# A graph kernel's attention layers: target scores spread behind the group's last sums

## The chip, the cores and the metric

The program runs on one core of a Trainium2 chip. The metric is device time in microseconds (us) of one execution; lower is better. A core has TensorE (PE: matmuls, PEld: its weight loads), VectorE (DVE), ScalarE (ACT), GpSimd (POOL, which here issues the gathers), SyncE (SP, which issues the other DMAs) and 16 DMA engines that all queues share.

## What is computed

Seven message-passing layers over a graph of 3125 nodes and 53125 edges, sorted by target node, with 256 features and layer norms between: one 8-head attention layer with edge features, four layers that sum or average, and two 4-head attention layers. The change touches only these last two:

```python
z = (x @ W).reshape(n, HEADS, ODIM)                  # HEADS = 4
el = jnp.sum(z * al, axis=-1)
er = jnp.sum(z * ar, axis=-1)
e = leaky_relu(el[src] + er[dst], negative_slope=0.2)
e_max = segment_max(e, dst, num_segments=n)
ex = exp(e - e_max[dst])
denom = segment_sum(ex, dst, num_segments=n)
msg = z[src] * (ex / denom[dst])[:, :, None]
out = segment_sum(msg, dst, num_segments=n) + x + b
```

## The kernel before

The edges are cut into 416 tiles of 128, and these into 52 groups of 8 tiles. A 4-head layer goes through its 52 groups in a software pipeline; each engine has its own program, in an order written out by hand, and the engines meet at semaphores.

**Gathers.** GpSimd issues eight indirect DMAs a group (L1819), one a tile. Each fetches 128 rows of 264 numbers (z and the source scores) from the layer's table into one of four row buffers. It waits for `rows_free`, which VectorE raises when a group has been added up (L1469). So, in step g, the buffer of group g-1 comes free, and the gathers of group g+3 start.

**Step g**, in which group g is summed and group g+1 is prepared:

- VectorE (`step` in `gat_dve`, L1471): `edge_scores(g+1)` adds the target scores, which lie in PSUM (`er_ps`), to the source scores in the gathered rows (L1387) and takes the leaky relu (L1388). It waits for the rows of group g+1 and for `er_ready`. Then the first half of `messages(g)` (L1425) multiplies z by the weights, once ScalarE has made them (`ex_ready`). `add_group(g-1)` adds the window of the group before (L1440, L1442), once TensorE has turned its sums (`sum_ready`), and raises `rows_free`. Then `scans(g+1)` (L1393, L1394: running maxima), the second half of `messages(g)`, `carry(g+1)` (L1400 to L1406: maxima that reach over tiles; waits for TensorE's L686), `rescale_node(g)` (L1434, L1436), `maxima(g+1)` (L1411 to L1417; the last one raises `shift_ready`) and `turned_hots(g+2)` (L1380).
- `turned_hots` compares the broadcast target numbers of a group's edges (`high_rows`, loaded by SP at L1740 with the tables of the group) with the partition number, and so makes the group's turned one-hots in bf16 (`turned_hot`, a part of the tile `attr`).
- TensorE (`step` in `gat_pe`, L741): `turn_scores(g+1)` (L681), the sums of group g over its eight tiles in three pieces (L711), between them `edges` (L686) and `carries` (L693) of group g+1, then `turn_back(g+1)` (L698), which turns the shifted scores for ScalarE and raises `back_ready`, then `spread_scores(g+2)` (L675): 24 matmuls of bf16, 8 tiles by 3 parts, with the turned one-hots as weights, which bring each edge's target scores into `er_ps`; the last raises `er_ready`. Then `rescales(g+1)` (L705), which waits for `ex_ready`, and `turn_sums(g)` (L724, L725), which raises `sum_ready`.
- ScalarE (`step` in `gat_act`, L1008): a copy for `near`, the one-hots of the sums, the copy of the group's sums (L1014, waits for the last L711), and `weights(g+1)`: L996, then the two exponentials L999 and L1000, which wait for `back_ready` and raise `ex_ready`.
- SP loads the tables of group g+3 once `maxima(g+1)` is done: penalties (L1733, L1737), then `high_rows` (L1740).

Of the kernel before, what the change touches and what calls it, by code (L numbers as in the profile page):

```python
# [82 lines left out]
def is_last(g):  # L83
    return isinstance(g, int) and g == NG - 1


def gnn_program(nc, a, out, stop):
    last_stage = NL - 1 if stop is None else stop
    ctx = ExitStack()
    with ctx:  # L90
# [252 lines left out]
        def wait_alone(eng, s, value):  # L343

            eng.wait_ge(s, value)
            eng.sem_inc(passed, 1)
# [110 lines left out]
        def tables_landed(eng, l, par, h):  # L457

            eng.wait_ge(seg_landed[par], SEG_BEFORE[l] + SEG_LOADS[l] * (h + 1))

        def next_group(j, h, ahead):

            return (j + ahead) % SUM_BUFS, h + (j + ahead) // SUM_BUFS

        def pair_of(j, h):

            return j % 2, 2 * h + j // 2
# [193 lines left out]
        def gat_pe(pe, l, turns, sum_turns):  # L661
# [6 lines left out]
            def spread_scores(n, j, h):  # L668

                par = j % 2  # L670
                pe.wait_ge(turned_hot_ready, gl + n + 1)
                pe.wait_ge(near_copied, gl + n + 1)
                for k in range(T):
                    for part in range(PARTS):
                        ins = mm(er_ps[:, k * H:(k + 1) * H], turned_hot[:, par, k, :],  # L675
                                 near[:, par, k, part * H:(part + 1) * H], start=part == 0, stop=part == PARTS - 1)
                ins.then_inc(er_ready, 1)

            def turn_scores(n):
                wait_alone(pe, al_ready, ag + n + 1)  # L680
                nc.tensor.transpose(alT_ps[0:TH, :], al3[:, 0:TH], ident[:, :]).then_inc(alT_ready, 1)  # L681

            def edges(n):
                wait_alone(pe, scans_ready, ag + n + 1)
                for j, ends in ((0, fwd[0:TH + 1, P - 1:P]), (1, bwd[0:TH + 1, 0:1])):
                    ins = mm(edge_ps[:, j * H * SLOTS:(j + 1) * H * SLOTS], ends,  # L686
                             perm[:, j, :, :].rearrange("p h s -> p (h s)"), start=True, stop=True)
                ins.then_inc(last_ready, 1)

            def carries(n):  # L690
                wait_alone(pe, carry_ready, ag + n + 1)
                for j in range(2):
                    ins = mm(carry_ps[0:TH, j:j + 1], carry_th[:, j, 0:TH], one[:, :], start=True, stop=True)  # L693
                ins.then_inc(carryT_ready, 1)

            def turn_back(n):
                wait_alone(pe, shift_ready, ag + n + 1)
                nc.tensor.transpose(back_ps[:, 0:TH], shifted[0:TH, :], ident[0:TH, 0:TH]).then_inc(back_ready, 1)  # L698

            def rescales(n, par):  # L700
                if not (isinstance(n, int) and n == 0):
                    pe.wait_ge(rescaled, ag + n)
                wait_alone(pe, ex_ready, ag + n + 1)
                for f in range(FC):
                    ins = mm(gat_resc_ps[:, f:f + 1], head_of[H][:, f, :], resc_h[par][0:H, :], start=True, stop=True)  # L705
                ins.then_inc(resc_ready, 1)

            def sum_tiles(par, b, ks):

                for k in ks:  # L710
                    ins = mm(gat_node_ps[par], gat_hot[par][:, k, :], src_rows(l, b)[:, k, 0:D + H],  # L711
                             start=k == 0, stop=k == T - 1)
                return ins

            def sums(g, b, half, ks):
                if ks[0] == 0:
                    pe.wait_ge(onehot_ready, ag + g + 1)
                pe.wait_ge(msg_ready, 2 * (ag + g) + half + 1)
                return sum_tiles(b % 2, b, ks)
# [7 lines left out]
            def turn_sums(g, b):  # L727
                par = b % 2
                pe.wait_ge(node_copied, NG * l + g + 1)
                pe.wait_ge(windows_done, NG * l + g - 1)  # L730
                turned(par).then_inc(sum_ready, 1)

                def window(w):
                    pe.wait_ge(more_ready, turns.now() + 1)
                    sum_tiles(par, b, range(T)).then_inc(more_nodes, 1)
                    pe.wait_ge(more_copied, sum_turns.now() + 1)
                    turned(par).then_inc(more_summed, 1)
                    turns.next()
                    sum_turns.next()
                further_windows(pe, g, window)  # L740

            def step(g, h, j):
                n = None if is_last(g) else g + 1
                if n is not None:
                    turn_scores(n)
                sums(g, j, 0, range(0, 4))
                if n is not None:
                    edges(n)
                sums(g, j, 1, range(4, 6))
                if n is not None:  # L750
                    carries(n)
                sum_tiles(j % 2, j, range(6, 8)).then_inc(node_ready, 1)
                if n is not None:
                    turn_back(n)
                    if not is_last(n):
                        spread_scores(n + 1, *next_group(j, h, 2))
                    rescales(n, (j + 1) % 2)
                turn_sums(g, j)

# [14 lines left out]
            spread_scores(1, 1, 0)  # L774
            rescales(0, 0)
            gat_loop(pe, step)

        def node_pe(pe, s):
# [588 lines left out]
        def gat_dve(dve, l, ch, turns, sum_turns):  # L1367
# [8 lines left out]
            def turned_hots(n, j, h):  # L1376

                par, turn = pair_of(j, h)
                tables_landed(dve, l, par, turn)
                V.tensor_scalar(turned_hot[:, par, :, :].rearrange("p t e -> p (t e)"), high_row[:, par, :], rank[:, 0:1],  # L1380
                                None, ALU.is_equal).then_inc(turned_hot_ready, 1)

            def edge_scores(n, b, h):

                rows_landed(dve, l, b, h)
                dve.wait_ge(er_ready, gl + n + 1)
                ch.then(V.tensor_tensor(grid(al), er_ps.rearrange("p (t h) -> p t h", h=H), src_rows(l, b)[:, :, D:D + H], ALU.add))  # L1387
                V.scalar_tensor_tensor(al3[:, 0:TH], al[:, 0:TH], 0.2, al[:, 0:TH], ALU.mult, ALU.max).then_inc(al_ready, 1)  # L1388
# [8 lines left out]
            def carry(n, par):  # L1397
                dve.wait_ge(last_ready, ag + n + 1)
                pr = gat_pen_row[0:1, par * 2 * HS:(par + 1) * 2 * HS]
                V.tensor_tensor_scan(carry_row[0:1, 0:HS], pr[:, 0:HS], edge_ps[:, 0:HS], -BIG, ALU.add, ALU.max)  # L1400
                ch.then(V.tensor_tensor_scan(carry_row[0:1, HS:2 * HS][:, ::-1], pr[:, HS:2 * HS][:, ::-1],
                                             edge_ps[:, HS:2 * HS][:, ::-1], -BIG, ALU.add, ALU.max))
                V.tensor_copy(perm[TH:TH + 1, 0, :, 0:1],
                              carry_row[0:1, 0:HS].rearrange("o (h s) -> o h s", h=H)[:, :, T:SLOTS])
                into = carry_row[0:1, 0:2 * (HS + 1)].rearrange("o (j x) -> o j x", j=2)[:, :, 0:HS]
                V.tensor_copy(carry_th[:, :, 0:TH].rearrange("o j (t h) -> o j h t", h=H),  # L1406
                              into.rearrange("o j (h s) -> o j h s", h=H)[:, :, :, 0:T]).then_inc(carry_ready, 1)
# [63 lines left out]
            def step(g, h, j):  # L1471
                n = None if is_last(g) else g + 1
                b, hn = next_group(j, h, 1)
                if n is not None:
                    edge_scores(n, b, hn)
                messages(g, j, 0)
                if not (isinstance(g, int) and g == 0):
                    add_group(g - 1, (j - 1) % 2)
                if n is not None:
                    scans(n, b % 2)  # L1480
                messages(g, j, 1)
                if n is not None:
                    carry(n, b % 2)
                rescale_node(g, j % 2)
                if n is not None:
                    maxima(n, b % 2)
                    if not is_last(n):
                        turned_hots(n + 1, *next_group(j, h, 2))

            edge_row = perm[TH:TH + 1, :, :, :]  # L1490
            V.memset(fwd[TH:TH + 1, :], 1.0)
# [10 lines left out]
            ch.flat()  # L1502

            gat_loop(dve, step, ch, GAT_STEPS)
            add_group(NG - 1, 1)

# [514 lines left out]
```

## Time and profile before

| | |
|---|---|
| median of 3 runs | 5965.95 us (5960.23 to 5992.97) |
| the profiled execution | 5953.5 us |
| its span | 5951.7 us |
| mean granted TensorE clock | 0.726 of full speed |
| busy: PE, PEld, DVE, ACT, POOL | 58%, 40%, 34%, 19%, 49% of the span |

Times in the rows are us from the span's start. The two 4-head layers run from about 4100 on: group after group, the first from 4144, the second from about 5045. An engine's name with a q behind it is its queue: DVEq L1469 is the semaphore increment of that line. Where a release is "remote", the profile found no instruction or DMA that gave it; "issue" means that the engine waited for nothing that the profile shows.

### The profile page before, as it was taken

To read this page: it belongs to the slowest core of one execution; us is meant where nothing else is said; L and a number is where in the kernel's file an instruction comes from. 1 tells how busy PE (TensorE), PEld (TensorE's weight loads), DVE (VectorE), ACT (ScalarE), POOL (GpSimd) and SP (SyncE) were. 2 spreads that over 40 slices of the span, in tenths; PEclk is the share of its full clock that TensorE was granted. 3 is DMA by queue.
4 is the path that set the end of the run, shared out by engine and by line. 5 is a ranking of instruction groups with operands and counts; after the bars stand their busy time and mean duration, and the time that the engine had idled before them with its cause. 6 is when DMAs were issued, how large, how long until landed. Compare 5 with 4: busy or idle time off the path is not lost.

```text
span 5951.7 us, 60656 instructions
## 1 busy us (share of the span) xinstructions
PE 3434.0 (58%) x14500; PEld 2353.8 (40%) x14501; DVE 2011.9 (34%) x4393; ACT 1158.3 (19%) x3026; POOL 2914.6 (49%) x3013
## 2 busy tenths in 40 slices
PE   4777777755556444454444744445656664665566
PEld 2554445434334333343333433333444443444343
DVE  3666666511111111111111411113444445444446
ACT  1333333210001000010000100004332333233233
POOL 2344444046664666646666266663544543454450
PEclk6887778777767777787667767777766666766766
DMA  5454545122222232222222122222333332333330
GB/s 170 141 145 139 143 137 145 35 75 87 81 84 71 87 90 85 85 82 87 86 81 82 55 87 84 86 83 64 94 90 92 92 87 66 89 91 91 91 93 24
DMA packets 280482, 546.80 MB, mean 92 GB/s; under 512 B 72515, under 2 KB 161655, under 8 KB 280223
## 3 DMA queue, kind: packets, MB, share of 16 engines
q0 software_dynamic: 140416, 391.24, 23.1%
q1 hardware_dynamic: 139807, 152.86, 8.5%
q14 instruction: 188, 1.54, 0.1%
q8 instruction: 71, 1.16, 0.1%
HBM read 512.47 MB, written 31.37 MB: 91 GB/s over the span
## 4 chain that ended last, share of the span: by engine, by line
another core or an unknown queue 39%; PE 32%; issue 11%; DVE 11%; ACT 3%; DVEq 2%; SPq 1%; DMA 1%; POOL 1%; ACTq 1%; POOLq 0%
PE ps L627 9%; PE ps L711 7%; PE ps L534 3%; PE ps L499 2%; PE ps L872 2%; DVE rows L1425 2%; PE ps L852 1%; PE ps L822 1%; PE ps L634 1%; PE ps L814 1%; DVE inv L1531 1%; ACT norm L1020 1%; ACT rows L1037 1%; PE ps L486 1%
## 5 line engine op out<-in xcount | busy, mean ns | idle before, releaser
L1819 POOL DMA_INDIRECT rows<-table,src_idx x2912 | 2875.5, 987 | 2709.0 <-issue 865.6
L627 PE MATMUL ps<-rows,attr 128*128 128x256 f32 x3328 | 1066.3, 490 | 188.6 <-issue 93.1
L627 PEld LDWEIGHTS ps<-rows,attr 128*128 128x128 f32 x3328 | 824.1, 254 | 394.7 <-issue 215.2
L1317 DVE TENSOR_TENSOR acc<-acc,ps 128x256 f32 x208 | 87.7, 422 | 2035.0 <-PE ps L634 1532.2
L634 PE MATMUL ps<-ident,rows 128*128 128x128 f32 x416 | 110.9, 356 | 1151.7 <-ACT rows L1037 931.6
L634 PEld LDWEIGHTS ps<-ident,rows 128*128 128x128 f32 x416 | 48.8, 165 | 1235.1 <-ACT rows L1037 984.5
L711 PE MATMUL ps<-rows,w_roots 128*128 128x260 f32 x832 | 329.5, 551 | 35.6 <-DVE rows L1425 35.3
L711 PE MATMUL ps<-rows,attr 128*128 128x260 f32 x832 | 325.0, 544 | 35.3 <-DVE rows L1425 35.3
L1353 DVE TENSOR_TENSOR attr<-iota,local 128x1024 f32<-128x1024 f32 x208 | 254.3, 1224 | 204.9 <-issue 136.2
L1037 ACT ACTIVATE rows<-ps,mean_of 128x256 f32<-128x256 f32 x156 | 73.8, 473 | 1240.2 <-remote 826.0
L499 PE MATMUL ps<-rT,attr 128*128 128x272 f32 x832 | 283.1, 470 | 52.3 <-DMA rT<-table 25.8
L534 PE MATMUL ps<-rows,rT 128*128 128x272 f32 x832 | 296.1, 514 | 7.0 <-DVE rows L1197 7.0
L681 PE MATMUL ps<-ident,al 128*32 128x128 f32 x104 | 38.3, 368 | 449.8 <-DVE al L1388 427.4
L711 PEld LDWEIGHTS ps<-rows,w_roots 128*128 128x128 f32 x832 | 212.4, 274 | 96.4 <-DVE rows L1425 39.4
L1425 DVE TENSOR_TENSOR rows<-rows,ps 128x1024 f32<-128x1024 f32 x208 | 249.2, 1198 | 2.6 <-ACT rows L1000 1.4
L1387 DVE TENSOR_TENSOR al<-ps,rows 128x32 f32<-128x32 f32 x104 | 19.9, 191 | 677.7 <-remote 671.7
L711 PEld LDWEIGHTS ps<-rows,attr 128*128 128x128 f32 x832 | 208.0, 269 | 94.3 <-DVE rows L1425 39.0
L534 PEld LDWEIGHTS ps<-rows,rT 128*128 128x128 f32 x832 | 197.5, 250 | 69.9 <-issue 15.6
L499 PEld LDWEIGHTS ps<-rT,attr 128*128 128x128 f32 x832 | 171.8, 224 | 117.8 <-issue 70.5
L1143 DVE TENSOR_TENSOR norm<-rT,ps 128x528 f32<-128x528 f32 x208 | 144.7, 696 | 177.4 <-PE ps L499 104.8
L681 PEld LDWEIGHTS ps<-ident,al 128*32 128x32 f32 x104 | 10.6, 102 | 482.1 <-issue 481.9
L988 ACT ACTIVATE w_roots<-iota,local 128x128 f32<-128x128 f32 x416 | 127.2, 388 | 378.4 <-DVEq L1468 378.4
(226 smaller groups left out, 4310.8 us busy)
## 6 DMA issues: line engine op xcount, KB each, us to landing
rT<-table SPq DMA_DIRECT2D x416, 136.0 KB
rows<-table,src_idx POOLq DMA_INDIRECT x2912
high_rows<-in_tiles SPq DMA_DIRECT2D x156, 256.0 KB
table<-rows SPq DMA_DIRECT2D x24, 512.0 KB, 2.9
table<-rows SPq DMA_DIRECT2D x12, 528.0 KB, 3.0
pens<-pen_rows SPq DMA_DIRECT2D x52, 96.2 KB
pens<-pen_rows SPq DMA_DIRECT2D x104, 48.1 KB
attr_parts<-acc SPq DMA_DIRECT2D x9, 416.0 KB
```

The lines of the kernel that those rows point to most:

```text
L499: ins = mm(ps[:, i, 0:TW], edge_turned[:, par, k, :], spans[:, k, :], start=True, stop=True)
L534: ins = mm(edge_node_ps[par], edge_hot[par][:, k, :], src_rows(l, b)[:, k, 0:TW], start=k == 0, stop=k == T - 1)
L627: ins = mm(node_ps[par % 2], sum_hot[:, par % 2, k, :], src_rows(l, par)[:, k, 0:D], start=k == 0, stop=k == T - 1)
L634: ins = nc.tensor.transpose(sum_ps[par % 2][f], node_sums[:, par % 2, f * P:(f + 1) * P], ident[:, :])
L711: ins = mm(gat_node_ps[par], gat_hot[par][:, k, :], src_rows(l, b)[:, k, 0:D + H], start=k == 0, stop=k == T - 1)
L872: ins = mm(into, x[:, f, k * P:(k + 1) * P], w_table[s + 1][:, f, 0:w], start=f == 0, stop=f == 1)
L988: ins = nc.scalar.activation(gat_hot[par][:, k, :], iota[:, 0:P], ACT.Abs, scale=-1.0, bias=local[:, bass.ds(g * T + k, 1)])
L1037: nc.scalar.activation(node_sums[:, par % 2, :], node_ps[par % 2], ACT.Copy, scale=mean_of[:, bass.ds(g, 1)] if l in MEAN_LAYERS else 1.0) ...
L1143: V.tensor_tensor(prod[:, q % 2, :, :], enc[:, q % 2, :, :], h_ps[:, :, H:TW], ALU.mult).then_inc(prod_ready, 1)
L1353: V.tensor_tensor(sum_hot[:, par % 2, :, :], iota[:, 0:P].unsqueeze(1).broadcast_to([P, T, P]), local[:, bass.ds(g * T, T)].unsqueeze(2).b ...
L1425: V.tensor_tensor(x[:, :, 0:D].rearrange("p t (h d) -> p t h d", h=H), x[:, :, 0:D].rearrange("p t (h d) -> p t h d", h=H), gat_ex_ps[b % ...
L1819: pool.indirect_dma_start(src_rows(l, par)[:, k, :], None, tables[l][:, :], bass.IndirectOffsetOnAxis(ap=src_idx[:, g * T + k:g * T + k + ...
```

## The change

Two calls are moved, and nothing else. On TensorE `spread_scores` goes ahead of `turn_back` in the step; on VectorE `turned_hots` goes from the end of the step to behind the second half of the messages. The calls ahead of the loop stay as they were.

```diff
@@ gat_pe, step
                 sum_tiles(j % 2, j, range(6, 8)).then_inc(node_ready, 1)
                 if n is not None:
-                    turn_back(n)
                     if not is_last(n):
                         spread_scores(n + 1, *next_group(j, h, 2))
+                    turn_back(n)
                     rescales(n, (j + 1) % 2)
                 turn_sums(g, j)
@@ gat_dve, step
                 messages(g, j, 1)
                 if n is not None:
+                    if not is_last(n):
+                        turned_hots(n + 1, *next_group(j, h, 2))
                     carry(n, b % 2)
                 rescale_node(g, j % 2)
                 if n is not None:
                     maxima(n, b % 2)
-                    if not is_last(n):
-                        turned_hots(n + 1, *next_group(j, h, 2))
```

TensorE, from the last sums of a step to its turned sums, before:

```order
L693 MATMUL ps<-one,carry_th 32x1 [waits carry_ready]
L693 MATMUL ps<-one,carry_th 32x1
L711 MATMUL ps<-rows,attr 128x260 x2
L698 MATMUL ps<-ident,shifted 128x32 [waits shift_ready]
L671 REGISTER_ALU
L675 MATMUL ps<-near,attr 128x4 [waits near_copied,turned_hot_ready]
L675 MATMUL ps<-near,attr 128x4 x23
L705 MATMUL ps<-resc_h,head_of 128x1 [waits rescaled,ex_ready]
L705 MATMUL ps<-resc_h,head_of 128x1
```

and with the change:

```order
L693 MATMUL ps<-one,carry_th 32x1 [waits carry_ready]
L693 MATMUL ps<-one,carry_th 32x1
L711 MATMUL ps<-rows,attr 128x260 x2
L671 REGISTER_ALU
L675 MATMUL ps<-near,attr 128x4 [waits near_copied,turned_hot_ready]
L675 MATMUL ps<-near,attr 128x4 x23
L698 MATMUL ps<-ident,shifted 128x32 [waits shift_ready]
L705 MATMUL ps<-resc_h,head_of 128x1 [waits rescaled,ex_ready]
L705 MATMUL ps<-resc_h,head_of 128x1
```

The 24 matmuls of L675 stand between the last sums (L711) and the transpose of the shifted scores (L698); L705 and L724 keep their places.

VectorE, the same step; `-` is before, `+` with the change:

```order
 L1394 SCALAR_TENSOR_TENSOR bwd<-pens,ps 32x128
 L1425 TENSOR_TENSOR rows<-rows,ps 128x4x256
+L1380 TENSOR_SCALAR attr<-high_rows,rank 128x1024 [waits seg_landed1]
 L1400 SCALAR_TENSOR_TENSOR carry_row<-gat_pen_row,ps 1x36 [waits last_ready]
 L1401 SCALAR_TENSOR_TENSOR carry_row<-gat_pen_row,ps 1x36
@@ -3383,5 +3384,4 @@
 L1416 TENSOR_TENSOR shifted<-ps,segmax 32x128 [waits dve_step]
 L1417 TENSOR_SCALAR rescale<-ps,segmax 4x1
-L1380 TENSOR_SCALAR attr<-high_rows,rank 128x1024 [waits seg_landed1]
 L1386 REGISTER_ALU [waits src_landed3]
 L1387 TENSOR_TENSOR al<-ps,rows 128x32 [waits er_ready]
```

The turned one-hots (L1380) stand ahead of the carry's first scan (L1400), where they stood behind the last row of the maxima (L1417).

## Rows read from the trace of the kernel before

**Rows 1.** Waits, both 4-head layers: who waited for whom, total us, times, longest.
```profile
DVE al L1387 <- remote: 671.7, 98, 46.0
...
DVE carry_row L1400 <- PE ps L686: 125.8, 93, 2.6
...
DVE al L1387 <- PE ps L675: 6.0, 6, 1.3
```

**Rows 2.** Timeline, a step without gathers: start, us, engine, line, operation [idle before].
```profile
4165.97 0.76 PE L675 MATMUL ps<-near,attr 128*128 128x4 bf16 x24
...
4166.83 0.19 DVE L1387 TENSOR_TENSOR al<-ps,rows 128x32 f32<-128x32 f32 x1 [0.92 <-PE ps L675]
```

**Rows 3.** Timeline, GpSimd's gathers, L675 and L1387 around the step that follows.
```profile
4150.73 0.95 POOL L1819 DMA_INDIRECT rows<-table,src_idx  x1 [0.30 <-issue]
...
4169.85 0.94 POOL L1819 DMA_INDIRECT rows<-table,src_idx  x1 [18.18 <-DVEq L1469]
...
4174.20 0.76 PE L675 MATMUL ps<-near,attr 128*128 128x4 bf16 x24
...
4179.03 0.95 POOL L1819 DMA_INDIRECT rows<-table,src_idx  x1 [0.30 <-issue]
4181.59 0.19 DVE L1387 TENSOR_TENSOR al<-ps,rows 128x32 f32<-128x32 f32 x1 [7.44 <-remote]
```

**Rows 4.** Windows: us, busy of PE, PEld, DVE, ACT, POOL, clock, DMA share, GB/s.
```profile
4161.00:4166.00 5.00, 4.41 (x21) 2.56 (x21) 2.66 (x12) 0.64 (x3) 0.00 (x0) 0.81 0.00 0
```

**Rows 5.** Timeline, a regular step in the second 4-head layer.
```profile
5113.67 0.02 SPq L1740 DMA_DIRECT2D high_rows<-in_tiles  x1
5113.93 0.19 DVE L1387 TENSOR_TENSOR al<-ps,rows 128x32 f32<-128x32 f32 x1 [6.01 <-remote]
...
5114.27 1.21 DVE L1425 TENSOR_TENSOR rows<-rows,ps 128x1024 f32<-128x1024 f32 x1
...
5115.40 0.27 DVE L1440 TENSOR_TENSOR den<-den,ps 4x128 f32 x1
...
5117.33 0.94 POOL L1819 DMA_INDIRECT rows<-table,src_idx  x1 [5.54 <-DVEq L1469]
5117.36 1.18 DVE L1425 TENSOR_TENSOR rows<-rows,ps 128x1024 f32<-128x1024 f32 x1
...
5121.70 0.39 ACT L1014 ACTIVATE w_roots<-ps 128x260 f32<-128x260 f32 x1 [1.48 <-PE ps L711]
...
5122.49 0.20 DVE L1417 TENSOR_SCALAR rescale<-ps,segmax 4x1 f32<-4x1 f32 x1
...
5122.62 0.47 DVE L1380 TENSOR_SCALAR attr<-high_rows,rank 128x1024 bf16<-128x1024 bf16 x1
5122.72 0.20 ACT L996 ACTIVATE resc_h<-rescale 4x1 f32<-4x1 f32 x1 [0.63 <-issue]
...
5122.84 0.21 PE L698 MATMUL ps<-ident,shifted 32*128 32x32 f32 x1 [1.17 <-issue]
5123.09 0.18 ACT L999 ACTIVATE ps<-ps 128x32 f32<-128x32 f32 x1 [0.16 <-PE ps L698]
...
5123.14 0.76 PE L675 MATMUL ps<-near,attr 128*128 128x4 bf16 x24
5123.18 0.19 ACT L1000 ACTIVATE rows<-ps 128x32 f32<-128x32 f32 x1
...
5123.83 0.60 PE L705 MATMUL ps<-resc_h,head_of 4*128 4x1 f32 x4
...
5124.64 0.27 PE L725 MATMUL ps<-ident,w_roots 128*4 128x128 f32 x1
...
5126.08 0.94 POOL L1819 DMA_INDIRECT rows<-table,src_idx  x1 [0.30 <-issue]
...
5129.24 0.19 DVE L1387 TENSOR_TENSOR al<-ps,rows 128x32 f32<-128x32 f32 x1 [6.16 <-remote]
```

**Rows 6.** DMA of all queues, 5116.2 to 5118.5.
```profile
DMA packets 0, 0.00 MB, mean 0 GB/s; under 512 B 0, under 2 KB 0, under 8 KB 0
```

## The prediction

> **What bounds the kernel now.** The change touches only the two 4-head layers, the last third of the program: 104 groups of 1024 edges, 52 a layer. So I read first the table of waits of that stretch, then the timeline of single steps. The longest wait there is VectorE's, ahead of the sum that opens a step (al, L1387): 671.7 us over 98 of the 104 groups, one of them 46 us long where a layer starts; the other 97 are about 6 us each. It is put down to a releaser that the profile doesn't know; in the six groups left it is TensorE's L675, together 6.0 us [rows 1].
>
> L1387 waits for two things: the gathered rows of its group, and er_ready, which the last of the 24 matmuls of L675 (spread_scores) gives. Which is it? In a step in which GpSimd issues nothing, L675 starts at 4165.97, takes 0.76, and L1387 follows 0.10 us after its end [rows 2]. In the next step [rows 3] L675 starts at 4174.20, so it ends about 4174.96, and L1387 starts only at 4181.59. Its rows (group 3) are not late: GpSimd had issued the first four groups by 4151.68 and then nothing until 4169.85, and the DMA engines stand at share 0.00 from 4161 to 4166 [rows 3, 4]. What is in flight at 4175 is group 4, which nobody needs yet. L1387 runs 1.6 us after the last issue of group 4 has ended (4179.98). A regular step says the same: L675 ends at 5123.90, the last gather is issued from 5126.08 to 5127.02, and L1387 starts at 5129.24, 5.3 us after the one and 2.2 us after the other [rows 5]. So **while gathers are in flight, what TensorE signals with L675 and behind it reaches the others only when those gathers are through**. Why, the profile doesn't show; that it does, the rows do. ScalarE's L999, which waits for the transpose just ahead of L675 (L698, 5122.84 to 5123.05), starts at 5123.09: that signal still passes at once.
>
> This closes a loop. From L1387 (call it zero, 5113.93) the messages start at 0.34 and the window sum of the group before (L1440) at 1.47; that frees a row buffer, GpSimd starts at 3.40, its eight gathers take until 13.09 (5127.02), and 2.2 us later L1387 runs again: a step of 15.31 us [rows 5]. Of these about 10 us are GpSimd's issue. VectorE has the old step's maxima done at 8.76 and the one-hots at 9.16, TensorE its last transpose at 10.98; both then wait.
>
> **The change part by part.** On TensorE the 24 matmuls of L675 move from behind L698 to ahead of it, right behind the group's last sums. On VectorE the one-hots that they load (L1380) move from the step's end to behind the second half of the messages. Nothing is added or removed, no DMA moves, and no queue of SP or GpSimd is passed.
>
> *L1380 on VectorE.* Removed from a place ahead of a 6 us wait, it gives nothing there. In its new place it stands ahead of the scan of the ends (carry, L1400), which waits for TensorE: 125.8 us over 93 groups, 1.35 each [rows 1], against 0.47 for L1380. It costs nothing, and 0.5 us at most if TensorE were no longer late; even that falls into the 6 us. Its new place asks for high_rows earlier: SP issues it at 5113.67 and in 5116.2 to 5118.5 no DMA packet of any kind moves, so it has landed by then, and the second messages end at 5118.54 [rows 5, 6]. No new wait.
>
> *L675 earlier on TensorE.* It could start when the last sums end. ScalarE's copy of them (L1014) starts at 5121.70 and L675 at 5123.14, so 1.4 us earlier at best; in the other step that I looked at it is 0.8. But er_ready follows the gathers, not L675: with these 97 steps as they are, this gives 0. In the six steps without gathers it gives up to 0.5 us each, because behind er_ready the messages wait for the weights too: 3 us together.
>
> *L698 behind L675.* This is the part that costs. Today the weights (L999, L1000) are ready long before L1387. Now L698 signals behind L675, so it is held as well. TensorE finishes its matmuls in order: "MATMULs are pc-monotone in start AND end — strict FIFO" (the Trainium skill, TensorE: Matmul & The Clock Gate, The mechanism); no row here shows a later matmul's signal overtaking an earlier one's. By rows alone: once both are released, ScalarE starts 0.04 after L698's end and takes 0.28 for L999 and L1000 (5123.09 to 5123.37), so the messages' weights stand at 0.32 and the messages start near 0.42 instead of 0.34. Behind these weights TensorE's L705 waits, and behind L705 the transposes L724 and L725, which took 1.08 together (5123.83 to 5124.91) [rows 5]. They now run after the release too: 0.42 + 1.08 = 1.50, and with 0.1 to 0.2 for the signal L1440 starts at 1.6 to 1.7 instead of 1.47. From below the cost is 0.08 (if only the messages move), from above 0.4 (if each of the four hand-overs takes 0.1 more). I take 0.25, since the transposes come out as last; GpSimd then starts 0.25 later and the whole loop with it: 97 x 0.25 = +24 us.
>
> *What follows.* TensorE's next sums start behind L705, L724, L725 and L681 rather than at 1.6, about 0.5 later, and all that VectorE does until 8.76 moves by as much. It lies in the 6 us of waiting and costs nothing. It also eats part of L675's lead: that burst then starts 0.3 to 1.0 us earlier in the step, not 1.4.
>
> **Sum:** +24 - 3 = +21 us. Made against the profiled execution, 5953.5 + 21 = 5974.5. The median of the three runs, 5965.95, lies 12.5 above that execution, so I forecast 5966 + 21 = **5987 us**, +0.35%. I take 0.5% (30 us) as what a measurement of this kernel can tell from no change.
>
> **Rivals.**
> *(a) The last sums are held too (slower).* Their signal, for which L1014 waits, comes directly ahead of the burst where today 0.8 to 1.4 us lie between. It decides if L1014 starts only with L1387. Then L1014 (0.39) and L996 stand ahead of L999 after the release, some 0.5 more: 97 x 0.75 - 3 = +70, 6036. For it: the burst starts as that signal leaves. Against: L698's stands just as close to it now and passes [rows 5]. 0.12.
> *(b) The release follows the burst (faster).* If it takes L675's own start plus a fixed time, and the end of the gathers is a coincidence, er_ready comes 0.3 to 1.0 earlier, say 0.75: 97 x (0.25 - 0.75) - 3 = -51, and with the full 1.0 it is -76: 5915 and 5890. Against: from burst end to L1387 it is 6.6 us in one of the two steps and 5.3 in the other, while from the gathers' last issue it is 1.6 and 2.2 [rows 3, 5]; neither is constant. 0.12.
> *(c) Nothing is held any more.* The burst might slip ahead of whatever holds it, as L698 does today 0.1 us earlier. Then GpSimd's issue alone sets the step: eight at 1.25, 10 us instead of 15.3, 97 x 5.3 = -514, 5452. It needs both L675 and L698 through. Against: gathers are in flight since 5117.33 and still at both places, 5.8 and 4.8 us into them [rows 5]. 0.06.
> *(d) It does nothing.* L1387 waits for its rows after all, or the hand-overs hide below L1425: 5966. By the Trainium skill the wait should not be L675's at all: a matmul's semaphore update is pushed once PSUM has acknowledged the bytes (Perfetto Trace Analysis, the TensorE instruction), so shortly after the end that the profile computes. The steps without gathers agree (0.10 us), the others do not [rows 2, 3]. 0.20.
> *Forecast* with its 0.08 to 0.4 a step (+5 to +36 us): 0.50.
>
> **How the numbers follow.** Slower by over 30 us: the upper third of the forecast (0.15), all of (a), and a little noise on (d): 0.29. Faster: (b), (c) and 0.03 of noise: 0.21. The rest, 0.50, within 0.5%. The range takes the forecast, (d), (a) at its 6036 and the near half of (b), with the 12 us by which runs of one kernel differ: 5935 to 6040. It leaves out (c), the far half of (b) and what lies above (a).
>
> **What would show it.** In the profile after: L675 starts 0.3 to 1.0 earlier counted from L1387, L698 directly behind it; L1387 still waits about 6 us for an unknown releaser and starts 1.6 to 2.2 us after GpSimd's last issue; L999 and L1000 just after L1387 instead of 6 us ahead; L705 and L724 after that; L1440 idle for TensorE's L725, about 0.2; a step of 15.5 to 15.6. It is wrong if L1387's wait is gone or belongs to L675 (b, c), if L1014 starts with L1387 (a), if L1380 waits for high_rows, or if L999 still runs within 0.5 us of L1417, which would mean that L698 is not held behind the burst.

## The result, and the profile after

The changed kernel takes **6074.19 us** (median of 4 runs, 6067.02 to 6079.98); the kernel before took 5964.59 beside it (4 runs). The ratio is 1.0178, 95% interval 1.0152 to 1.0203: slower by some 110 us, above the range given. Its profiled execution has a span of 6065.2 us against 5951.7, at a granted clock of 0.732 (0.726 before).

Where did the time come from? First the waits of both 4-head layers after the change (who waited for whom, total us, times, longest):

```profile
DVE al L1387 <- remote: 795.5, 98, 51.8
...
ACT ps L999 <- remote: 668.5, 95, 8.1
POOL rows L1819 <- DVEq L1469: 643.5, 96, 20.4
...
DVE den L1440 <- PE ps L725: 94.1, 98, 4.2
...
DVE fwd L1393 <- issue: 76.1, 100, 1.1
```

L1387's wait for an unknown releaser is still there, 795.5 us where it was 671.7 [rows 1]. New is ScalarE's, just as long: L999 waits for the signal of L698 and gets it at the same moment (the *release*). And L1440, which waited for TensorE in two steps before (7.4 us), now does in 98 (94.1 us), and GpSimd waits 643.5 for the row buffers instead of 543.1:

```profile
POOL rows L1819 <- DVEq L1469: 543.1, 96, 19.9
...
DVE den L1440 <- PE ps L725: 7.4, 2, 4.2
```

(those two are of the kernel before). One regular step after the change, timeline (start, us, engine, line, operation, idle time before and its releaser), to be held against [rows 5]:

```profile
5163.14 0.18 ACT L999 ACTIVATE ps<-ps 128x32 f32<-128x32 f32 x1 [7.50 <-remote]
5163.18 0.19 DVE L1387 TENSOR_TENSOR al<-ps,rows 128x32 f32<-128x32 f32 x1 [7.77 <-remote]
...
5163.53 0.98 PE L705 MATMUL ps<-resc_h,head_of 4*128 4x1 f32 x4 [7.76 <-ACT rows L1000]
...
5164.44 0.69 PE L724 MATMUL ps<-ident,w_roots 128*128 128x128 f32 x2
...
5164.92 0.42 PE L725 MATMUL ps<-ident,w_roots 128*4 128x128 f32 x1
...
5165.58 0.28 DVE L1440 TENSOR_TENSOR den<-den,ps 4x128 f32 x1 [0.73 <-PE ps L725]
...
5166.75 0.41 DVE L1393 TENSOR_TENSOR_SCAN fwd<-pens,ps 32x128 f32<-32x128 f32 x1 [0.56 <-issue]
...
5167.44 0.94 POOL L1819 DMA_INDIRECT rows<-table,src_idx  x1 [6.48 <-DVEq L1469]
...
5171.16 0.75 PE L675 MATMUL ps<-near,attr 128*128 128x4 bf16 x24
...
5171.36 0.39 ACT L1014 ACTIVATE w_roots<-ps 128x260 f32<-128x260 f32 x1 [1.15 <-issue]
...
5171.96 0.21 PE L698 MATMUL ps<-ident,shifted 32*128 32x32 f32 x1
...
5176.36 0.95 POOL L1819 DMA_INDIRECT rows<-table,src_idx  x1 [0.30 <-issue]
5179.53 0.19 DVE L1387 TENSOR_TENSOR al<-ps,rows 128x32 f32<-128x32 f32 x1 [7.72 <-remote]
```

The parts are as forecast: L698 ends at 5172.17 and is answered only at the release, which comes 2.2 us behind GpSimd's last issue (5177.31 to 5179.53); L1014, whose signal leaves directly ahead of the burst, is not held. The size is not. L705, L724 and L725 last from 5163.53 to 5165.34, 1.81 us, where they took 1.08 before [rows 5]. The windows say why (us, busy of PE, PEld, DVE, ACT, POOL with counts, granted clock, DMA share, GB/s), first before the change, then after it:

```profile
5123.80:5124.90 1.10, 1.10 (x11) 0.78 (x8) 0.00 (x0) 0.00 (x0) 0.79 (x2) 1.00 0.58 164
```
```profile
5155.80:5163.50 7.70, 0.00 (x0) 0.00 (x1) 0.29 (x2) 0.36 (x3) 3.94 (x5) 0.64 0.50 133
5163.50:5165.40 1.90, 1.87 (x9) 1.74 (x10) 1.32 (x2) 0.10 (x1) 0.00 (x0) 0.50 0.01 4
```

In their old place, behind the sums and the burst, they ran at clock 1.00 (2.4 GHz). In the new one they follow 7.7 us in which TensorE did nothing, and run at 0.50 (1.2 GHz). This holds for the whole stretch: from L705's start to L725's end it is 1.08 us in the median before, and 1.81 in 96 of the 102 steps after. The Trainium skill (TensorE: Matmul & The Clock Gate, What's actually happening) calls the lower clock the default that activity lifts; the trace agrees, 0.50 behind the idle time.

Medians over all steps, in us from L1387:

| | before | after |
|---|---|---|
| L1442 ends | 2.07 | 3.08 |
| GpSimd's first issue | 3.05 | 4.43 |
| its last issue ends | 13.04 | 14.37 |
| next L1387 | 15.20 | 16.36 |

From the first L1387 of a layer to its last, both layers together, it is 1528.0 before and 1626.2 after, +98.1: the 96 regular steps (those over 13 us) went from 15.30 to 16.43 on the average (+108.7), the six others gave back 10.5. Of the 15 us that the two spans differ by beyond this, 12.6 lie ahead of the first L1387, where nothing was changed.

### The profile page after: what moved, and what is told of

It is laid out like the page before. It is cut to its first block, busy times and chain, and to the rows that moved or that the text cites. A ratio compares the mean times of both kernels' runs of the same rounds, so it can differ in the third digit from the quotient of the medians.

```text
span 6065.2 us, 60656 instructions
## 1 busy us (share of the span) xinstructions
PE 3348.8 (55%) x14500; PEld 2357.6 (39%) x14501; DVE 2020.7 (33%) x4393; ACT 1161.5 (19%) x3026; POOL 2932.2 (48%) x3013
## 4 chain that ended last, share of the span: by engine, by line
another core or an unknown queue 35%; PE 32%; issue 15%; DVE 9%; ACT 3%; SPq 3%; DVEq 1%; DMA 1%; ACTq 1%; POOL 1%; POOLq 0%
PE ps L627 10%; PE ps L711 4%; PE ps L534 2%; PE ps L499 2%; PE ps L872 2%; PE ps L705 2%; PE ps L852 1%; PE ps L822 1%; PE ps L634 1%; PE ps L724 1%; PE ps L814 1%; DVE inv L1531 1%; DVE rows L1425 1%; ACT rows L1037 1%
## 5 line engine op out<-in xcount | busy, mean ns | idle before, releaser
L627 PE MATMUL ps<-rows,attr 128*128 128x256 f32 x3328 | 1021.4, 474 | 184.5 <-issue 102.7
L627 PEld LDWEIGHTS ps<-rows,attr 128*128 128x128 f32 x3328 | 792.1, 244 | 377.1 <-issue 217.6
L705 PE MATMUL ps<-resc_h,head_of 4*128 4x1 f32 x416 | 99.4, 339 | 699.8 <-ACT rows L1000 572.3
L705 PEld LDWEIGHTS ps<-resc_h,head_of 4*128 4x128 f32 x416 | 93.5, 309 | 708.2 <-issue 708.2
L1037 ACT ACTIVATE rows<-ps,mean_of 128x256 f32<-128x256 f32 x156 | 73.8, 473 | 1250.0 <-remote 727.0
L711 PE MATMUL ps<-rows,attr 128*128 128x260 f32 x832 | 301.4, 512 | 6.2 <-DVE rows L1425 5.7
L711 PE MATMUL ps<-rows,w_roots 128*128 128x260 f32 x832 | 300.5, 512 | 6.2 <-DVE rows L1425 4.6
L1387 DVE TENSOR_TENSOR al<-ps,rows 128x32 f32<-128x32 f32 x104 | 19.9, 191 | 798.7 <-remote 795.5
L1425 DVE TENSOR_TENSOR rows<-rows,ps 128x1024 f32<-128x1024 f32 x208 | 249.9, 1201 | 3.6 <-ACT rows L1000 1.8
L711 PEld LDWEIGHTS ps<-rows,w_roots 128*128 128x128 f32 x832 | 201.2, 259 | 52.7 <-DVE rows L1425 6.3
L711 PEld LDWEIGHTS ps<-rows,attr 128*128 128x128 f32 x832 | 200.1, 258 | 53.3 <-DVE rows L1425 7.3
L927 ACT ACTIVATE rT<-ps 128x512 f32<-128x512 f32 x208 | 123.9, 596 | 356.2 <-remote 127.4
```

What stands on the lines that cost most here:

```text
L627: ins = mm(node_ps[par % 2], sum_hot[:, par % 2, k, :], src_rows(l, par)[:, k, 0:D], start=k == 0, stop=k == T - 1)
L927: nc.scalar.activation(enc[:, q % 2, :, :].rearrange("p t (h d) -> p t h d", h=H)[:, :, :, 1:HEAD], enc_ps.rearrange("p t (h d) -> p t h d ...
L1037: nc.scalar.activation(node_sums[:, par % 2, :], node_ps[par % 2], ACT.Copy, scale=mean_of[:, bass.ds(g, 1)] if l in MEAN_LAYERS else 1.0) ...
L1425: V.tensor_tensor(x[:, :, 0:D].rearrange("p t (h d) -> p t h d", h=H), x[:, :, 0:D].rearrange("p t (h d) -> p t h d", h=H), gat_ex_ps[b % ...
```

## The experiments

In what follows, the *hold* is this: a signal of TensorE reaches the other engines late, by some us, while gathers are in flight.

**Theory 1**: the cost is what now stands between the release and L1440 (L705, L724, L725), and with it GpSimd's start. **Rivals**: the early one-hots cost by themselves; the hold has become longer since L698 is in it; the new order costs anywhere, hold or not.

The runs fell on different chips, and these are of two kinds. On three of them (and where the result was taken) the kernel before takes 5965 to 5976 us; on five others it takes **4767 to 4774**. Ratios are always to the kernel before on the same chip.

**1. One half alone (e1, e9).** VectorE's half of the change only:

```diff
                 messages(g, j, 1)
                 if n is not None:
+                    if not is_last(n):
+                        turned_hots(n + 1, *next_group(j, h, 2))
                     carry(n, b % 2)
...
-                    if not is_last(n):
-                        turned_hots(n + 1, *next_group(j, h, 2))
```

> Only VectorE's half of the change: the one-hots (L1380) stand behind the second messages, TensorE's order is that of the kernel before. Theory 1 (the cost comes from L705, L724 and L725, which in the changed kernel run between the release and the window sum L1440): no difference, 5966 within 15 us, and L1387 still about 6 us behind the end of the burst. Rival (the earlier one-hots themselves cost, by standing ahead of carry or by asking for high_rows early): most of the 110 us, 6050 or more, with L1400 later in the step.

> Only VectorE's half of the change, once more, for a chip that shows the hold. Theory 1: no difference, ratio 0.997 to 1.003; L1387 still starts about 2.2 us behind GpSimd's last issue. Rival (the early one-hots cost by themselves): 1.01 or more. On a chip without the hold: 0.998 as measured.

Measured: 0.9982 (0.9966 to 0.9997) on a chip of 4774, and 1.0001 (0.9971 to 1.0031) on one of 5976, with a median step of 15.18. The one-hots cost nothing; that rival falls.

**2. The turned sums ahead of the rescales (e2, e6), or ahead of the burst (e3).** From the changed kernel:

```diff
                     turn_back(n)
-                    rescales(n, (j + 1) % 2)
                 turn_sums(g, j)
+                if n is not None:
+                    rescales(n, (j + 1) % 2)
```

> The changed kernel, but TensorE turns the window sums (L724, L725) behind turn_back (L698) and ahead of the rescales (L705). L698 is still behind the burst and so still held; L724 and L725 need nothing of what is held, so they run inside the wait. Theory 1: L1440 follows L1425 again, rows_free comes about 1.3 us earlier than in the changed kernel, the step is 15.2 to 15.3 again, and the kernel takes 5955 to 5985. Rival (the hold itself has become longer or costlier since L698 and the exponentials are in it): no gain, 6060 to 6080.

> The changed kernel with the turned sums (L724, L725) ahead of the rescales (L705), once more, for a chip that shows the hold (the kernel of before takes 5965 there, its regular step 15.2). Theory 1 (in the changed kernel L705, L724 and L725 follow the release and so put off the window sum L1440 and with it GpSimd): L724 and L725 run inside the hold, rows_free comes about 1.4 us earlier than in the changed kernel, ratio to before 0.995 to 1.003. Rival (the hold itself is costlier since L698 is in it): 1.014 to 1.022. On a chip without the hold: 0.994 as measured.

On a chip of 5976: **1.0012 (0.9989 to 1.0035)**, where the changed kernel, on other chips of that kind, has 1.0178 and 1.0200. Its timeline (lines of VectorE and ScalarE stand one lower there, L1388 for L1387, L1441 for L1440):

```profile
5175.08 0.21 PE L698 MATMUL ps<-ident,shifted 32*128 32x32 f32 x1
...
5175.38 0.41 PE L724 MATMUL ps<-ident,w_roots 128*128 128x128 f32 x2
...
5175.63 0.27 PE L725 MATMUL ps<-ident,w_roots 128*4 128x128 f32 x1
...
5178.61 0.94 POOL L1820 DMA_INDIRECT rows<-table,src_idx  x1 [0.30 <-issue]
5181.49 0.19 DVE L1388 TENSOR_TENSOR al<-ps,rows 128x32 f32<-128x32 f32 x1 [6.55 <-remote]
5181.52 0.18 ACT L1000 ACTIVATE ps<-ps 128x32 f32<-128x32 f32 x1 [6.35 <-remote]
...
5181.91 0.98 PE L705 MATMUL ps<-resc_h,head_of 4*128 4x1 f32 x4 [6.01 <-ACT rows L1001]
5182.98 0.27 DVE L1441 TENSOR_TENSOR den<-den,ps 4x128 f32 x1
```

L698 is still behind the burst and still held, L705 still comes after the release at 0.98, but L724 and L725 are done inside the hold, in 0.5 instead of 0.9, and the window sum starts 1.49 behind L1388, as before the change (1.47). Median step 15.34 instead of 16.36. So theory 1 is shown, and the hold itself costs hardly more than it did (15.34 a step against 15.18 of the one-hots alone on the same chip). On a chip of 4774 the same order gives 0.9941 (0.9918 to 0.9964), 24 us less.

The third order, L724 and L725 directly behind the group's last sums, was run on the chip of 4774 only:

> The changed kernel, but TensorE turns the window sums (L724, L725) directly behind the group's last sums, ahead of the burst (L675). The burst then waits for ScalarE's copy of the sums and starts some 0.8 us later, near its place of before. Theory 1: as in the other order, 5955 to 5985, since L675's own start does not set the release. If the release follows the burst after all, some 0.5 to 0.8 us a step on top: 6000 to 6060. Rival (the hold is costlier in itself): 6060 to 6080.

1.0148 (1.0125 to 1.0171). TensorE waits there for ScalarE's copy of the sums (L1014), and the burst and L698 behind it start later (9.5 and 10.2 us behind L1387 in the median, 8.2 and 9.1 in the changed kernel on such a chip). It says nothing on the hold, which that chip does not show.

**3. The changed kernel again (e5, e17).**

> The changed kernel itself, on the chip that this call gets. The four runs before this one ran on a chip on which the kernel of before takes 4774, its steps 9.8 and GpSimd's issues follow each other without a wait for the window sum: there TensorE's signals are hardly held. Theory 1 (the 110 us are made of the hold, because the hand-overs behind L698 stand after its release): on a chip without the hold the change costs nothing and may gain, ratio 0.990 to 1.003; with the hold it costs 1.0152 to 1.0203 again. Rival (the new order costs on its own, by a later L698 and later exponentials, hold or not): ratio 1.01 to 1.02 on either chip.

> The changed kernel. On a chip with the hold (before near 5965): 1.0152 to 1.0245 as measured twice. On a chip without it (before near 4770), theory 1 (the cost is what stands between the release and L1440): nothing is held, L698 signals 0.7 us later than before but L675 1.4 us earlier, and the ratio is 0.993 to 1.003. Rival (the order costs by itself, since the exponentials and the rescales come 0.7 later): 1.005 to 1.02.

On a chip of 5969: 1.0200 (1.0154 to 1.0245), steps of 16.36 again. On one of 4770: **0.9976 (0.9966 to 0.9987)**, faster by some 11 us. From that one, timeline:

```profile
4410.22 0.75 PE L675 MATMUL ps<-near,attr 128*128 128x4 bf16 x24
...
4410.90 0.24 PE L698 MATMUL ps<-ident,shifted 32*128 32x32 f32 x1
4411.13 0.95 POOL L1819 DMA_INDIRECT rows<-table,src_idx  x1 [0.30 <-issue]
4411.18 0.18 ACT L999 ACTIVATE ps<-ps 128x32 f32<-128x32 f32 x1 [0.22 <-PE ps L698]
...
4411.52 0.19 DVE L1387 TENSOR_TENSOR al<-ps,rows 128x32 f32<-128x32 f32 x1 [0.79 <-DMA rows<-table,src_idx]
...
4411.57 0.57 PE L705 MATMUL ps<-resc_h,head_of 4*128 4x1 f32 x4 [0.42 <-ACT rows L1000]
...
4412.34 0.27 PE L725 MATMUL ps<-ident,w_roots 128*4 128x128 f32 x1
```

Here GpSimd issues without a pause, L698 is answered 0.04 after its end in the midst of the gathers, L1387 waits for its rows and not for TensorE, and the step is 9.9 us (median), about GpSimd's eight issues of 1.25. The same three lines in the same order, L705 to L725, take 1.04 us (4411.57 to 4412.61; 1.05 in the median) behind 0.42 of idling, at a granted clock of 1.00. So it is the clock that they find behind the long wait, and not their order, that makes them 1.81. The rival that the order costs by itself falls. The hold, then, is not the kernel's alone: some chips show it and some don't.

**4. What the hold hangs on (e7, e4, e8).** Half the gathers, in the kernel before (`GATHERS` is 4 in the 4-head layers and 8 in the others, and the waits for landed rows count by it):

```diff
-                    for k in range(T):
+                    for k in range(GATHERS[l]):
                         pool.indirect_dma_start(
```

> The kernel of before, but in the two 4-head layers GpSimd issues four gathers a group instead of eight (the source rows of tiles 4 to 7 are left as they were, so half of the messages is not the graph's). If the release follows GpSimd's last gather by about 2.2 us on a chip with the hold: the last issue ends near 8, release at about 10.2, which is just behind the burst, and the step falls from 15.2 to 10.2 to 10.8: some 450 to 500 us less. If the hold is a fixed time after the burst, or after the burst's matmuls whatever GpSimd does: the step stays at 15 and the kernel at 5950. On a chip without the hold the steps lose only what GpSimd's issue bounds, 9.8 to about 9.5.

This kernel leaves out half of the source rows, so it serves for its time alone. 5446.6 us on the chip of 5976 (one run): 530 less, median step 9.98. L1387's waits (L1388 there) now belong to TensorE's burst:

```profile
DVE al L1388 <- PE ps L676: 177.5, 96, 37.9
```

The last issue now ends 0.8 us before the burst starts, and L1388 follows the burst's end by 0.11 us (medians), where L1387 followed it by 5.2. So the hold needs gathers. Whether it is their issue or the traffic that they cause, the run doesn't part: it halves both.

The burst in the middle of the step, and no longer behind the last sums:

```diff
                 if n is not None:
                     edges(n)
+                    if not is_last(n):
+                        spread_scores(n + 1, *next_group(j, h, 2))
                 sums(g, j, 1, range(4, 6))
```

(with `turned_hots` behind `scans`).

> The burst (L675) is moved to the middle of the step, behind the matmuls of the ends (edges, L686) and ahead of the sums' second half, about 6 us after L1387 and 2.5 us after the first gather is issued; the one-hots (L1380) stand behind the scans. turn_back and the rescales keep their place of before. If what is held depends on how long the gathers have been in flight (signals of the first 9 us pass in both kernels): er_ready passes at about 6, L698 at about 9 as before, L1387's wait of 6 us is gone, the step falls to GpSimd's 10 us, and the kernel takes 5450 to 5550. If the burst itself opens the hold: everything of TensorE behind it is held until 2 us after GpSimd's last issue, carry, the sums and maxima come after that, and the step grows to about 20 us: 6350 to 6500. Theory 1 on the hand-over says nothing of this one.

> The burst (L675) in the middle of the step, behind the matmuls of the ends, once more, for a chip that shows the hold. If what is held depends on how long the gathers have been in flight (signals of the step's first 9 us pass in both kernels): er_ready passes near 6.5, L698 at 9 to 11 may be held or not; if it passes, the step falls towards 11 us and the kernel to 5500 to 5650. If the burst itself opens the hold: carry and the sums behind it are held until 2 us after GpSimd's last issue, the step grows to about 20 us, 6350 to 6500. On a chip without the hold: 1.015 as measured.

On a chip of 4774 it was 1.0150 (1.0122 to 1.0178), on one of 5976 1.0335 (1.0295 to 1.0375), 6172 us, with steps of 17.55: between the two forecasts. From its timeline:

```profile
5206.26 0.94 POOL L1819 DMA_INDIRECT rows<-table,src_idx  x1 [7.08 <-DVEq L1469]
...
5208.08 0.80 PE L675 MATMUL ps<-near,attr 128*128 128x4 bf16 x24
5208.87 0.21 DVE L1400 TENSOR_TENSOR_SCAN carry_row<-gat_pen_row,ps 1x36 f32<-1x36 f32 x1
...
5211.03 0.37 PE L693 MATMUL ps<-one,carry_th 1*32 1x1 f32 x4
...
5214.96 0.35 DVE L1414 SCALAR_TENSOR_TENSOR ps<-pens,ps 32x128 f32<-32x128 f32 x1 [4.38 <-remote]
5215.19 0.95 POOL L1819 DMA_INDIRECT rows<-table,src_idx  x1 [0.30 <-issue]
...
5217.84 0.39 ACT L1014 ACTIVATE w_roots<-ps 128x260 f32<-128x260 f32 x1 [8.81 <-remote]
```

L686's signal, ahead of the burst, passed (L1400 runs). L693's, 2 us behind the burst and 5 behind the first gather, was answered 3.6 us late (5211.40 to 5214.96). In the kernel before, L698's passes 5.7 us into the gathers [rows 5]. So the age of the gathers' run alone does not decide it. That a burst that meets gathers opens the hold, or adds to it, is the nearest reading, but argued: with its place and that of the one-hots much else shifts in the step. Besides, L1414 is let go *before* GpSimd's last issue, and L1014, one signal later, 1.7 behind it: the held signals leave one after the other, not all at the end.

**5. The burst out of the gathers' way (e10, e12, e14, e16), and thinned (e11, e13, e15).** In the first, `spread_scores` stands right behind `turn_scores`, ahead of the gathers of a regular step; one-hots, `near_group` and the load of `high_rows` are each made one group earlier:

```diff
                     turn_scores(n)
+                    if not is_last(n):
+                        spread_scores(n + 1, *next_group(j, h, 2))
                 sums(g, j, 0, range(0, 4))
...
-                        turned_hots(n + 1, *next_group(j, h, 2))
+                        turned_hots(n + 2, j + 3, next_group(j, h, 2))
```

> A version meant to beat both. The burst (L675) of the group after next stands right behind turn_scores (L681), about 1 us after L1387, where no gather is in flight in the steps with the hold (GpSimd starts at 3.05); for that the one-hots, the near scores (L1006) and the load of high_rows are each made one group earlier. Nothing else moves. On a chip with the hold: if only a burst that meets gathers opens a hold, the held signals go at once, L1387 follows VectorE's maxima, and steps fall towards GpSimd's 10 us; but then GpSimd issues almost without a pause and some bursts meet gathers again, so steps alternate: 11 to 14 on the average, 5550 to 5850 in all, 5450 if nothing is ever held. If any signal of TensorE later than some 9 us into the step is held, burst or not: L698 is, and the step stays at 15: 5950 to 6000. On a chip without the hold: GpSimd's issue sets the step anyway, ratio 0.993 to 1.003.

It fell three times on chips of 4768 to 4770, at 0.9996 (0.9985 to 1.0008), 1.0013 (0.9998 to 1.0028) and 1.0011 (0.9997 to 1.0024): nothing to gain where nothing is held. The fourth run fell on one of 5965:

> The burst (L675) ahead of the step's gathers, for a chip that shows the hold. Only a burst that meets gathers opens a hold: 11 to 14 us a step, 5550 to 5850. Any signal later than some 9 us into the step is held: 15, 5950 to 6000. Without the hold: 0.999 to 1.002 as measured.

**0.9873 (0.9835 to 0.9910)**, 5893 us: 73 us below the kernel before there, and some 180 below the changed kernel, which other chips of this kind ran. The step is 14.1 (median) instead of 15.2; both forecasts missed it, 5893 lies between them. The hold has moved (its lines: L1392 for L1387, L699 for L698, L1000 for L999, L676 for L675, L726 for L725, L1445 for L1440), in 70 steps (from the waits):

```profile
DVE den L1445 <- remote: 317.8, 70, 6.1
```

and the timeline of one of them:

```profile
5108.48 0.94 POOL L1841 DMA_INDIRECT rows<-table,src_idx  x1 [6.15 <-DVEq L1474]
...
5114.50 0.22 PE L699 MATMUL ps<-ident,shifted 32*128 32x32 f32 x1 [0.35 <-DVE rescale L1422]
5114.67 0.17 DVE L1392 TENSOR_TENSOR al<-ps,rows 128x32 f32<-128x32 f32 x1
...
5114.75 0.18 ACT L1000 ACTIVATE ps<-ps 128x32 f32<-128x32 f32 x1
...
5116.05 0.42 PE L726 MATMUL ps<-ident,w_roots 128*4 128x128 f32 x1
...
5116.95 0.78 PE L676 MATMUL ps<-near,attr 128*128 128x4 bf16 x24
5117.22 0.95 POOL L1841 DMA_INDIRECT rows<-table,src_idx  x1 [0.30 <-issue]
...
5120.43 0.28 DVE L1445 TENSOR_TENSOR den<-den,ps 4x128 f32 x1 [4.14 <-remote]
```

L1392 no longer waits, the step starts earlier, the last group's gathers are then still going, and now L726's signal is late: 4.0 us behind its end, and again 2.3 behind GpSimd's last issue (5118.17). L699's signal, 6.2 us into the gathers, still passed (5114.72 to 5114.75). L726's, 8.0 us into them, did not, and it was given 0.5 us ahead of this step's burst, with none between the two. So a hold can set in without a burst.

The thinned burst has 8 matmuls instead of 24 (`for part in range(1)`); it leaves out two of the three parts of the scores:

> The kernel of before with 8 matmuls in the burst (L675) instead of 24: only the first of the three bf16 parts of the near scores is multiplied, so the scores are rounded to bf16. On a chip with the hold: if it is the number of matmuls in quick succession that opens it, L1387 follows the burst's end and the kernel falls to 5450 to 5600; if it is any matmul of this kind while gathers are in flight, the step stays at 15.0 to 15.2, 5930 to 5970. On a chip without the hold: the step is shorter by at most the 0.5 us of the 16 matmuls where TensorE ends it, 0.995 to 1.0.

All three of its runs fell on chips without the hold (4766.5, 4761.1, 4765.6, against 4767 to 4770 before), so whether the number of matmuls opens the hold stays open.

**6. Both helpful edits together (e18).**

> The burst a group ahead, right behind turn_scores, and the turned sums (L724, L725) behind turn_back and ahead of the rescales (L705). On a chip with the hold: L725's signal leaves 0.6 to 1.0 us earlier, so fewer steps hold L1440, and the step falls from 14.1 to 12.5 to 13.8: ratio 0.96 to 0.985, against 0.987 without the second edit; if L725 is held in any case, since GpSimd's gathers run on beyond the step's start, 0.985 to 0.99. On a chip without the hold: the better of the two edits there, 0.993 to 1.0.

On a chip of 4770: 0.9992 (0.9979 to 1.0005). The gain of the turned sums' order alone (0.9941) is not in it. It was not run on a chip with the hold.

## Why the prediction was wrong

- **The hold, and what is held: right, for this order and these chips.** L1387 still follows GpSimd's last issue (2.0 us, median), L999 goes with L1387, L1014 is not held (rival a), nothing was freed (b, c), and it was not without effect (d). The burst starts 0.8 us earlier in the step, as forecast (9.28 to 8.48, medians). But as a rule, "what TensorE signals with L675 and behind it reaches the others only when those gathers are through" is too simple: with the burst moved, one signal was let go before the last issue, and another, ahead of the burst, was held (experiments 4 and 5).
- **L1380 costs nothing: right** (1.0001 and 0.9982).
- **The step that failed is the hand-over behind the release**, "the transposes L724 and L725, which took 1.08 together ... 0.42 + 1.08 = 1.50", and so "I take 0.25", with 0.4 as the upper end. It measured 1.13 us a step. The way was right, slower; the size was 21 us against 110. The chain was named rightly, its start too (L705 at 0.42 behind L1387, forecast and median), and priced with the durations of its old place, at clock 1.00 (the 1.08 is that of all three lines, L705 included); behind the hold TensorE is at 0.50 and it takes 1.81, 0.73 more. L1440 thus starts at 2.40 in the step shown instead of 1.65, where it had been at 1.47: +0.93 (+1.00 in the medians).
- **A second term was missing.** From the end of L1442 to GpSimd's first issue it was 0.98 and is 1.35. While L1440 had nothing to wait for, VectorE's queue could work ahead on the branches and increments behind it under the 1.2 us of L1425; now it can't, and L1393 sits idle 0.56 ahead instead of 0.33. That this is the reason is argued, not shown. Together GpSimd starts 1.38 later; 0.2 comes back between there and the next release.
- **The six steps without gathers** gave 10.5 instead of 3, but 6.3 of it is one step, the first of the first 4-head layer (12.4 to 6.1), and that looks like chance: the first step of a layer comes out anywhere from 6 to 12 with the same order (6.2 and 11.8 in the two layers of e5, 6.2 and 12.4 in e6). In e5 the six gave 4.5, close to the forecast.
- **The upper bound was no bound.** It let four hand-overs be 0.1 longer each and let no duration change. A row that would have given it is in the kernel before: there L705 too takes 0.98 instead of 0.60 in a step in which the granted clock was 0.50, after only 0.40 of idling (it was 1.00 from 4235 to 4238):

```profile
4238.20 0.98 PE L705 MATMUL ps<-resc_h,head_of 4*128 4x1 f32 x4 [0.40 <-issue]
```

and in the windows:

```profile
4238.20:4239.20 1.00, 1.00 (x5) 0.98 (x6) 0.00 (x0) 0.07 (x1) 0.94 (x1) 0.50 0.50 146
```

If every duration doubles at half the clock (an estimate; 1.08 became 1.81, 1.7 times), the three lines have 2.16 as their upper end, and 1.08 as their lower.

## What to carry to other kernels

Price a moved instruction at the clock of its new place: what is moved from behind a stream of matmuls to behind a wait can take much longer than in its old place (here 1.81 us instead of 1.08), and it counts in full if it stands between a release and what frees a buffer. Ahead of a wait that is needed anyway, place all that doesn't need what is waited for: here one exchange of two calls (turned sums ahead of rescales) took back the whole loss. And before an order is tuned around a stall that no releaser explains, run it on several chips; the kernel before takes 1200 us less on the five of the experiments' eight chips that don't show it.

## What the runs showed of the hardware

- **The same kernel takes 4770 or 5970 us, by the chip.** On the slow kind, TensorE's signals reach the others late while GpSimd's gathers are in flight, L698's by 7.4 in the step shown of the changed kernel (5172.17 to the release at 5179.53). It is not only in the 4-head layers: in the summing layers ScalarE's L1037 waits for an unknown releaser on the slow kind, and for TensorE's L627 on the fast. From the page of the kernel before, and of the one-hots alone on a chip of 4774:

```profile
L1037 ACT ACTIVATE rows<-ps,mean_of 128x256 f32<-128x256 f32 x156 | 73.8, 473 | 1240.2 <-remote 826.0
```
```profile
L1037 ACT ACTIVATE rows<-ps,mean_of 128x256 f32<-128x256 f32 x156 | 74.0, 474 | 1062.3 <-PE ps L627 1055.7
```

- By the Trainium skill (Perfetto Trace Analysis, the TensorE instruction) a matmul's update is pushed once PSUM has acknowledged its bytes. The fast kind agrees (in the changed kernel L999 starts 0.04 after L698's computed end, in every step of e17). The slow kind doesn't: there L999 starts 6.8 us after that end in the median, 8.0 at most.
- The held signals leave in order, mostly within 2.3 us after GpSimd's last issue, but in the run with the burst in mid-step one left before that issue. They are held with a burst ahead of them (L693 in e8, 5.1 us into the gathers), and also without one (L726 in e16, 8.0 us into them). Something that is worked off slowly while gathers run would look like this; which part of the chip it is, and whether the 24 quick matmuls feed it, the runs don't settle.
